# Self and cross attention of a four-block kernel: q, k and v from the third chunk on as products of rounded parts, and the transposes of a chunk behind its values

## The reference, cut to what matters

```python
def attention(q, k, v, mask):
    scores = jnp.einsum('bhqd,bhkd->bhqk', q, k) / jnp.sqrt(jnp.float32(HD))
    scores = scores * mask - 10000.0 * (1.0 - mask)
    probs = jax.nn.softmax(scores, axis=-1)
    return jnp.einsum('bhqk,bhkd->bhqd', probs, v)
...
# block 0, x: (32, 64, 256), enc: the context
qkv = layernorm(x) @ w_qkv + b_qkv          # (256, 768)
x = x + attention(...) @ w_ao + b_ao        # self, causal mask
q = layernorm(x) @ w_q + b_q                # (256, 256)
kv = enc @ w_kv + b_kv                      # (256, 512)
x = x + attention(...) @ w_co + b_co        # cross, pair mask
```

## Time and profile before

| what | value |
|---|---|
| median of 3 runs | 1943.7 us (1938.82 to 1943.97) |
| profiled execution, its time | 1946.16 us |
| profiled execution, its span | 1944.4 us |
| PE busy | 1855.2 us, 95% of the span |
| DVE, ACT, POOL busy | 57%, 54%, 51% |
| self and cross attention of block 0 | from 15 to about 250 us of the span |
| third attention | from about 1711 to 1850 us |

### The profile page before, as it was taken

How to read it: one execution, slowest core, us unless ns; L and a number is a source line. 1 busy time by engine, 2 the same in 40 slices (tenths; PEclk the granted TensorE clock), 3 DMA queues, 4 the chain that set the end, 5 groups by cost and what they waited for, 6 DMA issues and landing times.

```text
span 1944.4 us, 37701 instructions
## 1 busy us (share of the span) xinstructions
PE 1855.2 (95%) x14320; PEld 1507.0 (78%) x14320; DVE 1113.0 (57%) x2104; ACT 1042.5 (54%) x1945; POOL 998.8 (51%) x1140
## 2 busy tenths in 40 slices
PE   7999999989986999999999999999999998999899
PEld 5777789534454788888888888888888887967788
DVE  3656756389989555444444544544444545746654
ACT  4556543434344655665655656656665654345532
POOL 6777731376654544554554544544454535257620
PEclk9999999999998999999999999999999999999999
DMA  6000010000001223223223322322322310010000
GB/s 240 2 2 2 2 58 1 1 1 1 1 1 49 82 66 104 82 86 98 90 83 96 96 82 85 106 82 82 109 83 82 110 44 1 22 44 2 1 12 33
DMA packets 61842, 108.01 MB, mean 56 GB/s; under 512 B 7009, under 2 KB 42337, under 8 KB 60257
## 3 DMA queue, kind: packets, MB, share of 16 engines
q1 hardware_dynamic: 60784, 103.38, 16.9%
q10 hardware_dynamic: 880, 2.22, 0.3%
HBM read 103.47 MB, written 2.10 MB: 54 GB/s over the span
## 4 chain that ended last, share of the span: by engine, by line
PE 84%; DVE 7%; issue 3%; POOL 3%; ACT 2%; DMA 0%; DVEq 0%; SPq 0%; ACTq 0%; POOLq 0%
PE banks L864 18%; PE banks L935 9%; PE banks L892 9%; PE banks L471 7%; PE banks L629 7%; PE banks L646 6%; PE banks L924 6%; PE banks L905 3%; PE banks L480 3%; PE banks L528 2%; PE banks L553 2%; PE banks L539 2%; PE banks L510 2%; PE banks L465 2%; PE banks L913 1%
## 5 line engine op out<-in xcount | busy, mean ns | idle before, releaser
L1984 POOL TENSOR_TENSOR w_lo<-w2ring,w_hi 128x512 fp32r<-128x512 f32 x128 | 179.9, 1406 | 245.1 <-ACT w_hi L1130 245.1
L1806 DVE TENSOR_REDUCE nmax<-banks 128x4 f32<-128x260 f32 x128 | 54.2, 423 | 308.7 <-PE banks L905 308.7
L2067 POOL TENSOR_TENSOR wo_lo<-wo_ring,wo_hi 128x256 fp32r<-128x256 f32 x128 | 93.2, 737 | 250.6 <-ACT wo_hi L1338 250.4
L1794 DVE TENSOR_TENSOR v<-banks,dbv 128x512 f32<-128x512 f32 x128 | 88.5, 691 | 158.8 <-PE banks L892 158.7
L1338 ACT ACTIVATE wo_hi<-wo_ring 128x256 fp32r<-128x256 f32 x128 | 53.2, 417 | 190.3 <-PE banks L935 189.4
L935 PE MATMUL banks<-wo_hi,c_hi 128*128 128x256 f32 x512 | 149.0, 291 | 4.4 <-DVE c_lo L1799 4.4
L935 PE MATMUL banks<-wo_lo,c_hi 128*128 128x256 f32 x512 | 146.2, 286 | 0.0
L935 PE MATMUL banks<-wo_hi,c_lo 128*128 128x256 f32 x512 | 146.1, 285 | 0.0
L1325 ACT ACTIVATE k<-banks,cols 128x512 f32<-128x512 f32 x128 | 88.1, 689 | 80.4 <-PE banks L864 80.4
L924 PE MATMUL banks<-PT,v 128*128 128x128 f32 x1024 | 124.7, 275 | 1.0 <-issue 0.8
L924 PEld LDWEIGHTS banks<-PT,v 128*128 128x128 f32 x1024 | 119.7, 192 | 1.6 <-issue 1.2
(11 more groups left out here) (235 smaller groups left out, 5436.3 us busy)
## 6 DMA issues: line engine op xcount, KB each, us to landing
w2ring<-in_w SPq DMA_DIRECT2D x128, 384.0 KB, 3.2
b2ring<-in_b SPq DMA_DIRECT2D x128, 128.0 KB, 3.9
wo_ring<-in_wo SPq DMA_DIRECT2D x128, 128.0 KB, 3.4
mlp_w<-in_mlp SPq DMA_DIRECT2D x6, 1024.0 KB, 7.4
wl<-in_wres SPq DMA_DIRECT2D x1, 2688.0 KB, 8.8
X<-in_x_in SPq DMA_DIRECT2D x4, 512.0 KB, 11.3
wb<-in_wres SPq DMA_DIRECT2D x2, 1024.0 KB, 11.1
ctxT<-in_ctx_in SPq DMA_DIRECT2D x4, 512.0 KB, 18.4
```

What stands on the lines that cost most here:

```text
L1794: V.tensor_tensor(v2[i], held(("v2", v, i)).rearrange("p (s d) -> p s d", s=HV), dbv, ALU.add).then_inc(S["l2_v"], 1)
L1984: G.tensor_tensor(w2_lo[:, n % 2, :], w2ring[:, n % HR, 0:2 * KT * P], w2_hi[:, n % 2, :].bitcast(f32), ALU.subtract).then_inc(S["l2_wlo"], 1)
L2067: G.tensor_tensor(wo_lo[:, n % 2, :], wo_ring[:, n % WR, :], wo_hi[:, n % 2, :].bitcast(f32), ALU.subtract).then_inc(S["l2_wolo"], 1)
```

## The change

For chunks `ai` 2 to 7 (two of self attention, all four of cross attention) q, k and v are made as three products of rounded parts in place of plain fp32 matmuls. For this the weights of q, k and v are split once, in thirds: ACT copies 128x512 to fp32r and DVE subtracts, self attention's thirds in the units (ai, p) = (0,3), (1,0), (1,1), cross attention's in (2,0), (2,1), (3,0). The normed tokens of a chunk are split at p=2 of the chunk before (two copies on ACT, two subtracts on DVE), and the context's chunk at p=2 two chunks ahead on ACT and at p=0 of the chunk before on DVE. The new tiles lie where later MLP tiles are, so some waits are added: SP's load of the MLP's second weights waits until chunk 6 has made its values, and ACT and DVE wait in the MLP and at the end of attention for the last projections.

In all attention stages, the third one too, PE makes the values ahead of `front` at p=1, and DVE does values of group 0 ahead of `largest(n-1)` and those of group 1 behind it, where both groups stood behind it.

```diff
+def in_parts(ai):
+    return 1 < ai < 2 * CHUNKS
+
+def weights_part_at(ai, p):
+    return {(0, 3): (0, 0), (1, 0): (0, 1), (1, 1): (0, 2), (2, 0): (1, 0), (2, 1): (1, 1), (3, 0): (1, 2)}.get((ai, p))
@@ PE: project (values likewise, with w[5][y][2] and 256 columns) @@
+                        if in_parts(ai):
+                            src = source(ai, key)
+                            b = take(pe, ("qk", ai, n), "qk_T", 6 * ai + QK_DONE[n], among)
+                            pairs = [(x, y, k) for x, y in SPLIT for k in range(KT)]
+                            for x, y, k in pairs:
+                                last = mm(b, w[5][x][1 if key else 0][:, k, m * P:(m + 1) * P], src[y][:, k, :],
+                                          start=(x, y, k) == pairs[0], stop=(x, y, k) == pairs[-1])
+                            last.then_inc(S["qk_mm"], 1)
+                            return
@@ PE: the loop over units @@
                         if p == 1:
+                            for g in range(2):
+                                values(ai, g, among)
                             for k in range(KT):
                                 front(attended(ai) + 1, k, among)
-                            for g in range(2):
-                                values(ai, g, among)
@@ ACT @@
+                    def weights_part_hi(a, i):
+                        act.wait_ge((s_w0, s_w1)[a], 16)
+                        A(aw_hi[a][:, third(a, i)], aw_raw[a][:, third(a, i)], ACT.Copy).then_inc(S["at_whi"], 1)
+
+                    def normed_hi(ai):
+                        it = attended(ai)
+                        act.wait_ge(S["qk_mm"], 4 * ai)
+                        act.wait_ge(S["v_mm"], 2 * min(ai, CHUNKS))
+                        for k in range(KT):
+                            act.wait_ge(S["ln_hT"], KT * it + k + 1)
+                            A(ns[0][:, k, :], hT2[:, it % 2, k, :], ACT.Copy).then_inc(S["at_hhi"], 1)
...
+                        if weights_part_at(ai, p):
+                            weights_part_hi(*weights_part_at(ai, p))
+                        if p == 2:
+                            if in_parts(ai + 1):
+                                normed_hi(ai + 1)
+                            if CHUNKS <= ai + 2 < 2 * CHUNKS:
+                                attended_hi(ai + 2)
@@ DVE @@
+                    def normed_lo(ai):
+                        it = attended(ai)
+                        for k in range(KT):
+                            dve.wait_ge(S["at_hhi"], KT * (ai - 2) + k + 1)
+                            V.tensor_tensor(ns[1][:, k, :], hT2[:, it % 2, k, :], ns[0][:, k, :].bitcast(f32), ALU.subtract)\
+                                .then_inc(S["at_hlo"], 1)
...
                         scale(n)
+                        if p == 1:
+                            if ai - 2 >= start:
+                                dve.wait_ge(S["att_pv"], UNITS * (ai - 1))
+                            values(ai, 0)
                         if n > UNITS * start:
                             largest(n - 1)
                         if p == 1:
-                            if ai - 2 >= start:
-                                dve.wait_ge(S["att_pv"], UNITS * (ai - 1))
-                            for g in range(2):
-                                values(ai, g)
+                            values(ai, 1)
+                        if weights_part_at(ai, p):
+                            weights_part_lo(*weights_part_at(ai, p))
+                        if p == 0 and CHUNKS <= ai + 1 < 2 * CHUNKS:
+                            attended_lo(ai + 1)
+                        if p == 2 and in_parts(ai + 1):
+                            normed_lo(ai + 1)
@@ SP @@
                 mlp_weights_up(0)
+                sp.wait_ge(S["qk_mm"], 4 * (2 * CHUNKS - 1))
+                sp.wait_ge(S["v_mm"], 2 * (2 * CHUNKS - 1))
                 mlp_weights_down(0)
```

More of the change, by code:

```diff
@@ L227, in build @@
                 for n, w in (("h_hi", 0), ("h_lo", 1024))]
+        cs = [[view(at(f"c_{n}_a{p}", w + 1024 * i, KT * TOK, f32r), "p (k n) -> p k n", k=KT) for i, n in enumerate(("hi", "lo"))]
+              for p, w in enumerate((M + 2048, A + 16640))]
+        ns = [hs_a[i][1] for i in range(2)]
+        NQ = 3 * KT * D
+        aw_raw = [wa[:, 0:NQ], wb[:, 0:NQ]]
+        aw_hi = [at(f"aw_hi{a}", A + 20736 + NQ * a, NQ, f32r) for a in range(2)]
+        aw_lo = [at(f"aw_lo{a}", w, NQ, f32r) for a, w in enumerate((A + 23808, WB))]
+        assert A + 23808 + NQ <= SIZE
         L1S, L1N = WAT["L1_m1"][0], WAT["L1_W"][0] + WAT["L1_W"][1] - WAT["L1_m1"][0]
@@ L508, in values @@
                             t = 2 * g + i
+                            if in_parts(ai):
+                                pairs = [(x, y, k) for x, y in SPLIT for k in range(KT)]
+                                for x, y, k in pairs:
+                                    last = mm(b[:, i * D:(i + 1) * D], src[x][:, k, t * P:(t + 1) * P], w[5][y][2][:, k, :],
+                                              start=(x, y, k) == pairs[0], stop=(x, y, k) == pairs[-1])
+                                continue
                             for k in range(KT):
@@ L984, in _, with by_k @@
                 kv = part(wb, "L0_q", "L0_kv")
+                def by_k(w):
+                    return view(w, "p (k n) -> p k n", k=KT)
+                own2 = [[by_k(x)[:, :, i * D:(i + 1) * D] for i in range(3)] for x in (aw_hi[0], aw_lo[0])]
+                cross2_w = [[by_k(x[:, 0:KT * D])] + [by_k(x[:, KT * D:])[:, :, i * D:(i + 1) * D] for i in range(2)]
+                            for x in (aw_hi[1], aw_lo[1])]
                 w3 = part(wb, "L3_qkv", "L3_qkv", 1)[:, 0, :].rearrange("p (w k n) -> p w k n", w=3, k=KT)
-                run([attention(0, [(own[:, :, 0:D], own[:, :, D:2 * D], own[:, :, 2 * D:3 * D], part(wa, "L0_qkv", "L0_ao"), s_w0),
-                                   (part(wb, "L0_q", "L0_q"), kv[:, :, 0:D], kv[:, :, D:2 * D], part(wb, "L0_q", "L0_co"), s_w1)]),
+                run([attention(0, [(own[:, :, 0:D], own[:, :, D:2 * D], own[:, :, 2 * D:3 * D], part(wa, "L0_qkv", "L0_ao"), s_w0, own2),
+                                   (part(wb, "L0_q", "L0_q"), kv[:, :, 0:D], kv[:, :, D:2 * D], part(wb, "L0_q", "L0_co"), s_w1, cross2_w)]),
                      mlp(0), rwkv(), cross2(), mlp(1),
@@ L1101, in mlp @@
                     act.wait_ge(S["mlp_in2"], 16 * (m + 1))
+                    if m == 0:
+                        act.wait_ge(S["qk_mm"], 4 * 2 * CHUNKS)
+                        act.wait_ge(S["v_mm"], 2 * 2 * CHUNKS)
                     for n in range(CHUNKS * MT):
@@ L1586, in mlp @@
                         if i == 5 and c + 1 < CHUNKS:
+                            if m == 0 and c == 0:
+                                dve.wait_ge(S["qk_mm"], 4 * 2 * CHUNKS)
+                                dve.wait_ge(S["v_mm"], 2 * 2 * CHUNKS)
                             split(it + 1)
```

36 lines of the change are left out of this document (34 added, 2 removed).

## The result

The changed kernel takes 1952.43 us (median of four runs, 1952.14 to 1953.84) where the kernel before took 1941.26 beside it (four runs, 1938.76 to 1943.97). The ratio is 1.0059, interval [1.004, 1.0078]: 11 us slower, where 8 us faster was forecast, and outside the forecast's whole range of 1931.0 to 1942.0. A second measurement, in the last set of experiments, gave 1952.73 against 1941.02, ratio 1.006 [1.0047, 1.0073].

The account below looks back on a forecast made before the run. The prediction took PE to bound the kernel. Its gain of 11.8 us less 0.3, 0.6, 1.0, 0.8 and 1.15 left 7.95, say 8 us: 1935.7 us from a median of 1943.7, range 1931.0 to 1942.0.

Parts of the forecast that it names:

- The price of the products: PE in chunks 2 to 7: cheaper projections and values save 1.97 us a chunk, 11.8 us over six chunks.
- the side of the costs: Amounts taken off the gain: 0.3 last cross chunk, 0.6 contention, 1.0 and 0.8 self attention's start, 1.15 third attention.
- Step (1): Chain through `largest` behind half the values: subtractions meeting POOL cost 0.1 us of PE wait a chunk, 0.6 in all.
- rival B: POOL and DVE slow each other in every chunk, PE waits 0.8 us each; 1939.95 us, chance 0.24.
- the ring of banks: At p=1, `weigh` claims group 0's bank 4.74 us after `scores`; DVE has read it at 3.96, so no wait.
- It costs nothing unless the work stands in a chain ... Three chains are not: Added ACT copies and DVE subtracts hide in free time, except in three chains: `largest`, self attention's start, third attention.
- Step (2): Start of self attention: `scores` of unit 4 starts 1.5 us later; 1.0 us kept, plus 0.8 for the clock.
- at even odds: New idle ahead of unit 4 may bring a second half-pace stretch of 1.6 us; 0.8 us put for it.
- Step (3): Third attention gets only the order: second transpose waits for its bank, `scores(2)` later; 1.15 us, bounds 0 and 2.8.
- Rival C: Slower: chain slips, PE idles 1.1 us before `scores` every chunk, clock drops; 1951 us, chance 0.09 with other losses.

Follow-up runs that it names:

- e3: Changed kernel with the subtractions of tokens and attended rows cut to 8 of 512 columns once each buffer was filled; 1945.34 us, ratio 1.0026.
- e9: Changed kernel with self attention's weight parts made before its first chunk, cross attention's rounded at (0,2) and subtracted at (1,0), (1,1), (2,0); 1942.94 us, ratio 1.0007.
- e4: Changed kernel with VectorE's subtractions of the weights one unit later, ScalarE's rounding left in place; 1947.93 us, ratio 1.004.
- e8: The kernel before, unchanged, run once more for a second profile; 1938.55 us, span 1936.7.
- e6: Changed kernel with the old order at the second unit of a chunk in the third attention alone; 1947.66 us, ratio 1.0035.
- e7: Changed kernel with e9's moved weight parts, e5's merged subtractions, and the new order only in chunks with products in parts; 1935.51 us, ratio 0.9973.
- e10: e7 with tokens rounded right behind ScalarE's evictions at the second unit and subtracted ahead of `largest` at the third; 1934.95 us, ratio 0.9965.
- e2: Changed kernel with the old order on both engines, so products in parts only; 1946.12 us, ratio 1.003.
- e5: Changed kernel with each pair of VectorE subtractions of tokens and attended rows made one instruction of 128x1024; 1948.21 us, ratio 1.0041.
- e1: The kernel before with the new order only, no products in parts; 1947.23 us, ratio 1.0037.

## Why the prediction was wrong

**The price of the products was right.** Values 2.96 for a forecast of about 2.95, and 26.04 us a cross chunk in e3 for 26.0 to 26.1. The 1.97 a chunk is real: 27.98 − 26.04 = 1.94. What failed is on the side of the costs, 3.85 us in the prediction; with the gain of 11.8 and a loss of 11.7 they would have to come to 23.5.

**Step (1), contention: the mechanism was named and its size was wrong.** The prediction read two subtractions in 2.35 us as "about 0.5" for each and put 0.1 us a chunk. At that place GpSimd ran two instructions of 2.04 us together. Beside the additions of 1.9 to 2.4 us the pair took 4.95. The price is what is left of GpSimd's instruction, paid again by each VectorE instruction that GpSimd's next one gets ahead of. A cross chunk lost 26.80 − 26.04 = 0.76, what rival B had as its upper bound (0.8), and the first projection in parts waited 2.72 in e9. Taking the columns away (e3) is worth 6.6 us where 0.6 was put. Nor was the wait the expected one: the prediction said that the ring of banks holds, and asked for a wait for `kbd` or `qT`; after's cross chunks wait for the bank that the late addition to X reads. What bears on this stood beside the term in the prediction, as a general contention, from the Trainium skill's GPSIMD Engine Reference, section Key points; read as a lock for a whole instruction it would have asked which GpSimd instruction runs at that place.

**"It costs nothing unless the work stands in a chain ... Three chains are not" missed a fourth.** VectorE's subtractions of weights were counted as 0.69 each in free time. VectorE takes its queue in order, and the one at the first unit of a chunk waits for ScalarE's copy, which stands behind `kbd`, `qT` and the four normalisations. VectorE stands 5.8 to 6.0 us three times over, and the `scale` behind it comes 2.5 to 5.0 late. This is the step that failed: it was worth no term in the sum. Together with the copy on ScalarE at unit 4 it is the largest, 10.3 by e9; moving the subtractions alone (e4) gives 3.9 of it, and how the rest divides wasn't separated.

**Step (2), the start, was right as a mechanism and too small.** The copy of 0.62 and the later `largest` did put `scores` of unit 4 back, from 42.02 to 43.37, near the 43.5 forecast, and a second half-pace stretch came, as "at even odds". The prediction ended there with 1.8 us. After it came further stretches at the lower clock, 10.2 us of them from 64.9 on and 6.8 from 119.5, behind waits that the first two points made. And the price of a stretch was read from one execution: behind the wait of 1.11 the prediction found half pace, but in e8 the same wait (at 59.27) is followed by `turn` in 1.09 and the projections in 3.60, at the full clock.

**Step (3), the third attention: right place, a quarter of the size.** 1.15 was put; `scores(2)` came 1.6 later against its stage's start, the half-pace stretch that was there already doubled (6.6 us and more for 3.4), and the whole is 4.1 by the traces and 4.9 by e6's ratio. The bound of 2.8 (a half-pace stretch on top) was too low as well.

**The sign.** Rival C, slower, at a chance of 0.09 with the other losses, had the right end, 1951, by luck: it let the chain slip in every chunk. No cross chunk idled 1.1 us as C asked, and the cross chunks won time. The loss lies in the four chunks of self attention (13.2 in the traces, 10.4 of it in chunks 1 to 3) and in the third attention (4.1). The profile had what was needed for the missed step: ScalarE's order in the first units, and an in-order wait to be asked for each moved or added instruction.

**Left open.** By the ratios the removals sum to 10.3 (weights) + 4.9 (third attention) + 6.6 (subtractions) = 21.8 of the 23.5; each is rough, they may overlap, and the rest wasn't separated. The cross chunk of e7 stays half a microsecond above e3's by a wait for `qT`; what makes `qT` late there wasn't tested, only that e10's move of the subtraction doesn't help. The clock's part was not measured by itself, since it moves with the waits: in self attention e2 loses 9.6 us with one stretch of about 3.4 at the lower clock from 44 us on, where after loses 13.2 with 20.4 us of them.

## What to carry to other kernels

For every wait that a change adds, ask where the producer stands in its own queue at that moment, and what stands behind the consumer: work of 0.7 us in "free time" held an engine for 6 us and what stood behind it for 2.5 to 5. Between VectorE and GpSimd count instructions, not columns: merge small ones with two SBUF inputs, and put them where GpSimd is idle or its instruction is about to end (that last was shown to shorten the subtraction in e10, not the kernel). An order that is made for new, shorter products should be applied only where they are. And read a price, of the clock above all, from more than one trace.

## What the runs showed of the hardware

Two subtractions of 8 columns with two SBUF inputs ended with GpSimd's addition beside them, 2.19 us for both, or with its second one, 3.97 us (e3). Behind one subtraction of 1024 columns GpSimd's next addition took 2.88 instead of 1.90 (e5). The same program gave spans of 1944.4 and 1936.7 us, with stretches of 3.2 us and more at granted clock 0.52 in the one and 1.00 in the other. The clock is also not decided by the waits just ahead of it alone: unit 4 waited 0.79 us for `qT` in e1 and in e9, and the next stretch was at 0.70 on the mean in e1, against 1.00 in e9. The row of e1:

```profile
43.80:49.00 5.20, 5.20 (x15) 3.13 (x15) 2.22 (x2) 1.98 (x4) 3.80 (x5) 0.70 0.02 3
```
